# Another order of the steps in a software-pipelined recurrence: PE, VectorE, ScalarE, GpSimd and the DMA queue

## What is computed

```python
xa = ln(x);  sx = shifted(xa) - xa;  xxx = xa + sx*maa_x
m = einsum(tanh(xxx @ maa_w1), maa_w2)            # five adapters: w, k, v, r, g
xj = xa + sx*(maa_j + m_j)                        # five mixed inputs
w = exp(-exp(time_decay + tanh(xw @ decay_w1) @ decay_w2))
r, k, v = xr @ Wr.T, xk @ Wk.T, xv @ Wv.T;  g = silu(xg @ Wg.T)
for each token:  a = k v^T;  out = r . (faaaa*a + s);  s = a + w*s
y = head_norm(out)*gn_w + gn_b
x = x + (y*g) @ Wo.T                              # residual
xc = ln(x);  sxc = shifted(xc) - xc               # second shift
x = x + sigmoid((xc + sxc*fmaa_r) @ fWr.T) * (relu((xc + sxc*fmaa_k) @ fWk.T)**2 @ fWv.T)
```

## Time and profile before

| | before |
|---|---|
| median of three runs | 907.3 us |
| the profiled execution | 907.18 us |
| its span on the core | 905.4 us |
| PE busy / DVE busy / ACT busy / POOL busy | 857.8 / 567.1 / 429.4 / 228.5 us |
| start of `whole_y` of sequences 0, 3 and 7 | 73.99, 202.79 and 374.12 us |

### The profile page before, as it was taken

The page is one execution under the profiler, slowest core; times in us unless marked ns, Lnnn a source line. Parts: engine busy times, 40 slices in busy tenths (PEclk is TensorE's granted clock), DMA queues, the critical chain, the costliest instruction groups (busy, mean ns, idle before and its releaser), DMA issues.

```text
span 905.4 us, 16349 instructions
## 1 busy us (share of the span) xinstructions
PE 857.8 (95%) x6220; PEld 671.0 (74%) x6220; DVE 567.1 (63%) x1318; ACT 429.4 (47%) x965; POOL 228.5 (25%) x242
## 2 busy tenths in 40 slices
PE   6777999999999988999999999999989999999998
PEld 5766777686867765676787777877767677888987
DVE  3499999999999989552233453333434365544654
ACT  3313242424242445344666685757656885333342
POOL 3546556464646458200000000000000000110100
PEclk9988999999999999999999999999999999999999
DMA  7657645554637253104002020202140231000200
GB/s 272 164 117 207 186 138 148 147 150 134 158 114 189 81 153 78 49 19 106 18 9 86 9 63 1 63 1 63 30 185 1 105 133 64 1 0 0 82 0 35
DMA packets 44421, 80.51 MB, mean 89 GB/s; under 512 B 21485, under 2 KB 27629, under 8 KB 42558
## 3 DMA queue, kind: packets, MB, share of 16 engines
q1 hardware_dynamic: 39742, 77.71, 29.8%
q10 hardware_dynamic: 4608, 1.84, 0.8%
HBM read 70.36 MB, written 9.18 MB: 88 GB/s over the span
## 4 chain that ended last, share of the span: by engine, by line
PE 46%; ACT 3%; DMA 1%; issue 1%; DVE 1%; SPq 0%; DVEq 0%
PE bank L1856 9%; PE bank L1843 8%; PE bank L1717 8%; PE bank L1723 7%; PE bank L1809 4%; PE bank L1801 3%; PE bank L1828 3%; PE bank L1765 2%; PE bank L1751 2%; ACT smb L1300 2%; DMA cx<-latc_scratch 1%; ACT pts L1308 1%; PE bank L1475 0%; PE bank L1817 0%; ACT cx_hi L1190 0%
## 5 line engine op out<-in xcount | busy, mean ns | idle before, releaser
L900 DVE CUSTOM_DVE_ANT_0 smb<-bank,mask 112x487 f32<-112x487 f32 x128 | 78.1, 660 | 126.1 <-issue 126.0
L693 DVE TENSOR_TENSOR_SCAN scan<-bank,scan 128x448 f32<-128x448 f32 x128 | 132.0, 1073 | 5.8 <-POOL scan L547 4.9
L1481 PEld LDWEIGHTS bank<-xj,front 128*128 128x128 f32 x1024 | 119.6, 196 | 10.1 <-issue 8.1
L544 POOL TENSOR_TENSOR scan<-scan,ks 128x896 f32<-128x896 f32 x64 | 124.2, 1940 | 2.3 <-DMA scan<-v_scratch 2.2
L1481 PE MATMUL bank<-xj,front 128*128 128x112 f32 x1024 | 121.9, 280 | 1.5 <-POOL xj L535 1.5
L1300 ACT ACTIVATE smb<-smb,nmax 112x487 f32<-112x487 f32 x128 | 88.3, 691 | 64.9 <-DVE nmax L900 64.5
L521 POOL TENSOR_TENSOR small<-small,neghalf 112x1 f32<-112x1 f32 x24 | 13.4, 559 | 362.4 <-DVE small L936 268.1
L700 DVE TENSOR_TENSOR scan<-scan,bank 128x896 f32<-128x896 f32 x64 | 68.8, 1078 | 1.8 <-PE bank L1481 1.0
L535 POOL TENSOR_TENSOR xj<-tmp,xa 128x448 f32<-128x448 f32 x40 | 42.4, 1062 | 86.1 <-DVE tmp L662 86.1
L1121 ACT ACTIVATE bank<-ws 128x448 f32<-128x448 f32 x32 | 17.5, 548 | 91.1 <-DVE scan L693 77.2
L1809 PE MATMUL bank<-ident,smb 112*122 112x112 f32 x512 | 56.6, 262 | 3.9 <-ACT smb L1300 3.5
(11 more groups left out here) (196 smaller groups left out, 1760.8 us busy)
## 6 DMA issues: line engine op xcount, KB each, us to landing
scan<-v_scratch SPq DMA_DIRECT2D x64, 448.0 KB, 5.5
cx<-in_ctxt SPq DMA_DIRECT2D x8, 750.0 KB, 5.2
raw_w<-in_wbig SPq DMA_DIRECT2D x4, 1024.0 KB, 7.8
w<-in_w SPq DMA_DIRECT2D x2, 2048.0 KB, 7.4
w<-in_w SPq DMA_DIRECT2D x1, 3328.0 KB, 11.7
tail<-in_wbig SPq DMA_DIRECT2D x3, 1024.0 KB, 9.2
front<-in_wbig SPq DMA_DIRECT2D x2, 1024.0 KB, 9.9
x_f<-in_x SPq DMA_DIRECT2D x8, 224.0 KB, 6.3
```

The costliest lines, as they stand in the source:

```text
L544: g.tensor_tensor(buf[:, :, :], buf[:, :, :], ks[b % 2][:, k:k + 1, 0:T].broadcast_to([P, VS, T]), ALU.mult).then_inc(s["a_ready"], 1)
L693: n = v.tensor_tensor_scan(flat, decay, flat, 0.0, ALU.mult, ALU.add)
L900: v.tensor_tensor_reduce(sm[r], bank[r][0:T, 0:NKEY], mask_b[b % 2][:, :], -1.0 / DH, 3e38, ALU.add, ALU.min, nmax[:, h:h + 1]).then_inc(s ...
L1481: i = t_.matmul(tiles(dst)[:, m, :], w[:, k, m * P:(m + 1) * P], x[:, k, :], start=k == 0, stop=k == NT - 1)
```

## The change

The order of the calls in `period` is another one on PE, DVE, ACT, POOL and SP. No instruction's operands change, and none is added or taken away except one wait: `own_token` now also waits for `y_ready` of the sequence before. Core of the diff (SP, POOL, DVE and ACT; PE's is of the same kind):

```diff
@@ SP
             def period(i):
                 if 0 <= i < B:
-                    chunk(i, 2)
+                    chunk(i, 4)
                     chunk(i, 3)
-                    chunk(i, 4)
                     chunk(i, 5)
...
                 if 0 <= i < B:
                     chunk(i, 6)
+                if 1 <= i < B:
+                    load_residual(i)
+                if i == B - 1:
+                    load_context(1)
+                if 0 <= i - 2 < B - 2:
+                    store_columns(i - 2)
+                if 0 <= i < B:
                     chunk(i, 7)
                 if i == 0:
                     norm_vectors(1, "gn_b")
                 if i == 1:
                     tail_weight(3, "wr_loaded")
-                if 0 <= i - 2 < B - 2:
-                    store_columns(i - 2)
-                if 0 < i < B:
-                    load_residual(i)
-                if i == B - 1:
-                    load_context(1)
+                if 0 <= i - 2 < B - 1:
+                    store_latents(i - 2)
                 if 0 <= i + 1 < B:
                     store_values(i + 1)
                     chunk(i + 1, 0)
+                    chunk(i + 1, 2)
                     chunk(i + 1, 1)
@@ DVE
             def own_token(b):
                 dve.wait_ge(s["pr_ready"], b + 1)
                 dve.wait_ge(s["ks_ready"], b + 1)
+                wait(dve, "y_ready", b)
...
                 if 0 <= i < B:
+                    own_token(i)
+                    scan_chunk(i, 1)
+                    times_r(i, 0)
                     times_r(i, 1)
+                    scan_chunk(i, 2)
+                    scan_chunk(i, 3)
+                if 0 <= i - 1 < B:
+                    centred(i - 1)
+                if 0 <= i - 2 < B - 1:
+                    gated_values(i - 2)
+                    latents(i - 2)
+                if 0 <= i + 1 < B:
+                    shift(i + 1)
                     shifted(i + 1)
                 if 0 <= i < B:
+                    scan_chunk(i, 4)
+                if 0 <= i - 1 < B - 1:
+                    inverse_deviation(i - 1)
+                    group_norm(i - 1)
+                if 0 <= i < B:
+                    gating(i)
                     times_r(i, 2)
                 if 0 <= i - 1 < B - 1:
                     gated(i - 1)
...
                 if 0 <= i - 1 < B - 1:
                     residual(i - 1)
                 if 0 <= i < B:
-                    times_r(i, 5)
+                    times_r(i, 4)
+                if 0 <= i + 2 < B:
+                    norm_first(i + 2)
                 if 0 <= i - 1 < B - 1:
                     norm_end(2, rows_t, x2, "x2n_ready", i - 1)
                 if 0 <= i < B:
+                    times_r(i, 5)
                     scan_chunk(i, 6)
+                if 0 <= i - 1 < B - 1:
+                    second_shift(i - 1)
@@ ACT
-                if 0 <= i + 1 < B:
-                    values(i + 1)
-                    store_second_values(i + 1)
                 if 0 <= i < B:
                     decays(i, 3)
...
                 if i == B - 2:
                     context_high(0)
                 if 0 <= i + 1 < B:
-                    keys(i + 1)
-                if i == B - 2:
-                    weight_high(0)
+                    values(i + 1)
+                    store_second_values(i + 1)
                 if 0 <= i - 1 < B - 1:
                     second_columns(i - 1)
...
                     decay_tanh(i + 1)
+                    keys(i + 1)
+                if i == B - 2:
+                    weight_high(0)
@@ POOL
                 if 0 <= i < B:
                     scan_input(i, 6)
-                    scan_input(i, 7)
                 if 0 <= i + 1 < B:
                     mixed(i + 1, MIX_W)
                 if 0 <= i - 1 < B - 1:
                     rstd(2, i - 1)
+                if 0 <= i + 2 < B:
+                    rstd(1, i + 2)
+                if 0 <= i < B:
+                    scan_input(i, 7)
```

More of the change, by code:

```diff
@@ L795, in period @@
                     gating(i)
-                    scan_chunk(i, 4)
+                    times_r(i, 2)
                 if 0 <= i - 1 < B - 1:
                     gated(i - 1)
-                if 0 <= i + 1 < B:
-                    mix(i + 1, MIX_V)
                 if i + 1 == B:
@@ L804, in period @@
                     v.memset(cx[1][:, :, NKEY:PAD], 0.0).then_inc(s["pad_ready"], 1)
+                if 0 <= i + 1 < B:
+                    mix(i + 1, MIX_V)
+                    mix(i + 1, MIX_K)
                 if 0 <= i < B:
                     own_values(i)
-                if 0 <= i + 1 < B:
-                    mix(i + 1, MIX_K)
-                if 0 <= i < B:
+                    scan_chunk(i, 5)
                     times_r(i, 3)
-                    scan_chunk(i, 5)
                 if 0 <= i + 1 < B:
                     mix(i + 1, MIX_W)
-                if 0 <= i < B:
-                    times_r(i, 4)
                 if 0 <= i - 1 < B - 1:
@@ L822, in period @@
                 if 0 <= i < B:
+                    times_r(i, 5)
                     scan_chunk(i, 6)
-                if 0 <= i + 2 < B:
-                    norm_end(1, rows_f, x_f, "xn_ready", i + 2)
                 if 0 <= i - 1 < B - 1:
                     second_shift(i - 1)
+                if 0 <= i < B:
+                    times_r(i, 6)
+                if 0 <= i - 1 < B - 1:
                     channel_mix(i - 1, 0)
                 if 0 <= i < B:
-                    times_r(i, 6)
+                    scan_chunk(i, 7)
                 if 0 <= i + 1 < B:
@@ L840, in period @@
                 if 0 <= i + 1 < B:
-                    scan_chunk(i + 1, 0)
+                    mix(i + 1, MIX_G)
+                if 0 <= i + 2 < B:
+                    norm_end(1, rows_f, x_f, "xn_ready", i + 2)
                 if 0 <= i < B:
@@ L847, in period @@
                 if 0 <= i + 1 < B:
-                    scan_chunk(i + 1, 1)
-                    times_r(i + 1, 0)
-                    scan_chunk(i + 1, 2)
-                    own_token(i + 1)
-                    scan_chunk(i + 1, 3)
-                if 0 <= i + 2 < B:
-                    shift(i + 2)
-                if 0 <= i - 1 < B - 1:
-                    gated_values(i - 1)
-                if 0 <= i < B:
-                    centred(i)
-                if 0 <= i - 1 < B - 1:
-                    latents(i - 1)
+                    scan_chunk(i + 1, 0)
             def last_period():
@@ L1638, in period @@
                     spare_products(12)
-                if i == 0:
-                    sum_pair(0, 0)
+                if 0 <= i - 1 < B - 1:
+                    variances(i - 1)
+                if 0 <= i - 2 < B - 2:
+                    latents_turned(i - 2)
+                if 0 <= i < B:
+                    sum_pair(i, 0)
                 if 0 <= i + 1 < B:
                     adapter_inputs(i + 1)
-                if 0 < i < B:
-                    sum_pair(i, 0)
+                if 0 <= i < B:
+                    own_sums(i)
                 if 0 <= i + 1 < B:
@@ L1657, in period @@
                 if 0 <= i + 1 < B:
+                    value_product(i + 1)
                     key_product(i + 1)
```

65 lines of the change are left out of this document (21 added, 44 removed).

## The result

The changed kernel takes 923.67 us (median of four runs, 918.53 to 926.70), the kernel before on the same chip 907.77: a ratio of 1.016, 95% interval 1.0097 to 1.0223. The forecast was 908.6, its range ended at 918. The profiled execution of the changed kernel took 925.09 with a span of 923.4.

A forecast was written before the change was run, and what follows sets the result against it. DVE and PE were taken as both nearly full in steady periods, with slack at the ends. Fill +1.5, weight +0.3, period 1 0, periods 2 to 5 +3.2, period 6 -3.6, period 7 0: +1.4, 908.6 us, range 901 to 918.

The forecast's parts named there:

- The added wait: DVE's wait for `y_ready` in `own_token`: cost 0, since a whole scan pair lies between.
- Head norm: DVE's 0.45 us wait before the reciprocal goes, a new 0.25 comes before `gated`: -0.2 a period.
- Chunk 7, the meeting: Late-loaded chunk 7: POOL's product meets DVE's `second_shift` on SBUF, 1.0 a period; with head norm +3.2 over periods 2 to 5.
- The 0.2 for period 1: Meeting's cost in period 1, where chunk 7 comes 0.6 earlier without `store_columns`: about 0.2, period sum 0.
- Period 6: DVE's 3.75 us wait for `second_columns` goes; 4.83 idle becomes 0.25 plus a meeting of 1.0: -3.6.
- Period 7: Earlier norm of x2 takes up to 1 us from PE's waits, chunk 7 lands later: 0, between -1.5 and +2.
- Fill: Start of the pipeline: sequence 0 about 0, period 1 +1.5 for `own_token` waiting on the receptance product.
- +1.5 for period 1: `own_token` stands behind one chunk only and waits for a receptance product of 5.45 us: +1.5, 0 at 3.83.
- The weight: 1 MB weight load ahead of the v store in SP's queue, period 1: some 2.5 us, mostly covered, +0.3.
- The forecast's sign: Whole kernel: slightly slower, sum +1.4 us on the profiled 907.18.
- Rival C: Slower: in steady periods `second_shift` waits the whole product and v stores finish later, 2.5 a period, +13.4, 920.6; chance 0.18.

The follow-up runs named there:

- experiment 7: The changed kernel with chunk 7 back right behind chunk 6 and the 1 MB weight back ahead of the wait for residual: 915.61 us, 1.0067.
- experiment 10: The kernel of experiment 7 plus products that nobody reads in PE's waits of period 0: 912.11 us, 1.0030.
- experiment 6: The kernel before, with only the 1 MB weight moved behind the wait for residual, just ahead of sequence 2's v stores: 909.13 us, 0.9997.
- experiment 8: The kernel before, with only ACT's order of period 6 changed (context work ahead of values, weight work behind the decay's tanh): 905.41 us, 0.9974.
- experiment 2: The changed kernel with the 1 MB weight put back ahead of the wait for residual in SP's queue: 918.44 us, 1.0114.

## Why the prediction was wrong, step by step

- *The added wait*: 0 was right. Where `own_token` waits, it waits for PE's receptance product.
- *Head norm*: -0.2 a period was right in kind; 0.45 is gone, `gated` waits 0.29 to 0.40 where 0.25 was taken.
- *Chunk 7, the meeting*: the mechanism was right, its frequency not. In the profiled execution DVE was held once for the whole rest of the product (1.9 us, period 2), and in periods 3 to 5 DVE came first. Periods 4 and 5 take 43.56 and 43.57 with chunk 7 late, 43.17 and 43.35 with it early (experiment 7): 0.2 to 0.4 a period, where 0.8 was summed. The 0.2 for period 1 was right (0.86 in place of 0.61).
- *Period 6*: -3.6 taken, 46.14 to 42.75 measured, -3.4. Right in the sum, in part by luck: the 1.0 in it for a meeting did not come; the scan of chunk 7 waited 0.74 for its late load instead, and `second_shift` 0.21 for ACT.
- *Period 7*: taken as 0 (-1.5 to +2), measured +3.8. This step failed. I wrote that chunk 7 "lands some us later" behind the context and gave it no price of its own; it held DVE for 4.86. Behind it stood PE's clock (5.38 us for 3.69; DVE waited 1.97 at `residual` for it), and, once the load is early, the meeting of `rows_t` with POOL.
- *Fill*: +1.5 taken, +6.9 to y(0) and +2.1 in period 1 measured. This step failed too, at "For sequence 0 ... about 0"; its +1.5 for period 1 was near, with `own_token` waiting 2.71 for a receptance product of 5.95. I counted the other products at the durations of the old trace, though the new order changes when PE waits. Value and key products took 10.50 for 7.40; with PE kept at work y(0) comes 4.8 earlier (experiment 10), and of the 5.8 us that experiment 7 still loses ahead of y(0) 1.0 is left.
- *The weight*: +0.3 taken ("most of it covered"). SP's wait for the stores grew by 4.3, and DVE waited 3.5; y(1) to y(2) lost 6.7, with 1.9 of it in the meeting and 1.2 in a wait for PE at `whole_y`. Period 3 lost 1.7 in the wake of it, 0.89 of that in `own_token`'s wait for PE. The cover was there in the old order (experiment 6), not in the new one.

The forecast's sign was right, which is little for a sum of +1.4, and its size wrong by about 15 us. Rival C named the right side, but its place, the steady periods, was the wrong one: periods 4 and 5 hardly lost. By the medians mending the queue gives 8 us back, keeping PE at work 7, one meeting taken away 2, and the new order is then level with before (0.9991). Its one gain, period 6, can be had without the rest: experiment 8 is 0.26% under the kernel before (0.9953 to 0.9995).

Open stays whether weight and chunk 7 really give less together (8.1) than singly (5.2 and 8.5): executions of one kernel differ by some 10 us here, in experiment 2 from 912.16 to 922.93, and its profiled one had the old 7.40 for value and key products.

## What to carry to other kernels

A transfer moved behind a wait in an in-order queue takes everything behind it along: price the landing of the next load, not only its issue, and check the cover in the new order, not in the old one. Where an engine's clock can fall while it waits, durations read from the old trace hold only as long as the waits do, so ends of a pipeline need a price for the same work at the lower level. Of two instructions that hold each other up, let the one off the path start second, if need be by a wait.

## What was not expected of the hardware

The wait directly ahead does not settle PE's clock: behind 1.54 and 1.52 us idle the output product took 3.69, behind 1.54 and 1.53 it took 6.65 (experiment 7). In the profiled executions it took 3.69 in the old order each time (four kernels), and 5.08 to 6.68 in all eight kernels of the new order without products ahead of it. In the fill the same instructions took 10.50 in one execution (the changed kernel) and 7.40 in another (experiment 2), behind idle times of 2.27 in both. What else decides was not tried. And `rows_t`, with one tensor as input, was held by POOL just as `second_shift` with two (2.03 for 0.54); the prediction had counted on two-operand instructions only. The Trainium skill (SBUF — State Buffer, section "Who interferes with whom") names `tensor_scalar` among the instructions that can take the shared port, and the row agrees.
